# Bilinear gather by matmul: image differences, clamped-ramp weights and 32x32 row sums in place of absolute-distance weights and 128x128 row sums

## The reference

```
py = clip(row + off[..., 0], 0, 31);  px = clip(col + off[..., 1], 0, 31)
out = v00*(1-wy)*(1-wx) + v01*(1-wy)*wx + v10*wy*(1-wx) + v11*wy*wx
```

## Time and profile before

| | us |
|---|---|
| median of 3 runs | 6671.31 (6658.63 to 6683.49) |
| the profiled execution, first to last instruction | 6663.4 |
| TensorE busy (matmuls) | 5906.7 (89%) |
| VectorE busy | 4273.1 (64%) |
| ScalarE busy | 2369.6 (36%) |
| GpSimd busy | 348.5 (5%) |

### The profile page before, as it was taken

One profiled execution on the slowest core, in us unless ns is written; L12 is line 12 of the kernel. 1 busy time (PEld: TensorE's weight loads), 2 busy tenths in 40 slices (PEclk: granted clock), 3 DMA queues, 4 the chain that ended last, 5 costly groups with the idle time before them and its releaser, 6 DMA issues. The chain is left out here.

```text
span 6663.4 us, 63932 instructions
## 1 busy us (share of the span) xinstructions
PE 5906.7 (89%) x22480; PEld 3405.5 (51%) x22528; DVE 4273.1 (64%) x6238; ACT 2369.6 (36%) x2515; POOL 348.5 (5%) x193
## 2 busy tenths in 40 slices
PE   4877888769998999898997999999999969978997
PEld 2333333247776776676774444444444434434442
DVE  5888888856655665221223777778778747746774
ACT  2222222022221221000001666666666626634651
POOL 0222222300000000000000000000000000000000
PEclk7888888679998999999998999999999989989997
DMA  0000000010000000222124002011020060044012
GB/s 27 19 20 19 20 19 19 13 64 13 13 7 20 13 13 24 88 51 64 45 57 108 5 5 69 5 30 46 5 69 5 5 161 23 5 62 95 6 36 84
DMA packets 237972, 242.27 MB, mean 36 GB/s; under 512 B 176425, under 2 KB 178025, under 8 KB 236745
## 3 DMA queue, kind: packets, MB, share of 16 engines
q1 hardware_dynamic: 237640, 237.98, 13.1%
HBM read 137.28 MB, written 100.66 MB: 36 GB/s over the span
## 5 line engine op out<-in xcount | busy, mean ns | idle before, releaser
L1349 ACT ACTIVATE g_wts<-ps,l_index 128x1024 f32<-128x1024 f32 x1536 | 1712.0, 1115 | 1812.3 <-PE ps L1384 1810.4
L1397 PE MATMUL ps<-g_wts,l_img 128*128 128x512 f32 x3072 | 1577.8, 595 | 19.2 <-DMA l_img<-dense 19.1
L1384 PE MATMUL ps<-g_coord,l_spread 128*128 128x512 f32 x3072 | 1479.9, 563 | 107.6 <-DMA g_coord<-coords 106.3
L1369 DVE TENSOR_TENSOR g_prod<-ps,g_wts 128x512 f32<-128x512 f32 x1536 | 1062.7, 692 | 538.2 <-issue 439.5
L1361 DVE TENSOR_SCALAR g_wts<-g_wts 128x1024 f32<-128x1024 f32 x1536 | 1050.4, 684 | 76.2 <-ACT g_wts L1349 76.2
L1384 PEld LDWEIGHTS ps<-g_coord,l_spread 128*128 128x128 f32 x3072 | 556.9, 191 | 986.0 <-issue 567.6
L1279 PE MATMUL ps<-o_pad,o_ow 128*128 128x512 f32 x3456 | 849.9, 408 | 7.7 <-DVE o_pad L821 7.7
L1092 PE MATMUL ps<-l_pair,l_w 128*128 128x512 f32 x3072 | 782.1, 404 | 0.0
L1279 PEld LDWEIGHTS ps<-o_pad,o_ow 128*128 128x128 f32 x3456 | 657.0, 190 | 195.0 <-DVE o_pad L821 7.9
L1397 PEld LDWEIGHTS ps<-g_wts,l_img 128*128 128x128 f32 x3072 | 577.4, 189 | 170.7 <-DMA l_img<-dense 23.4
L1092 PEld LDWEIGHTS ps<-l_pair,l_w 128*128 128x128 f32 x3072 | 576.6, 191 | 157.0 <-issue 29.4
(11 more groups left out here) (240 smaller groups left out, 4312.7 us busy)
## 6 DMA issues: line engine op xcount, KB each, us to landing
coords<-o_parts SPq DMA_DIRECT2D x192, 256.0 KB, 3.8
g_coord<-coords SPq DMA_DIRECT2D x18, 2048.0 KB, 9.6
l_x<-xcur SPq DMA_DIRECT2D x16, 1024.0 KB, 6.3
l_img<-dense SPq DMA_DIRECT2D x96, 128.0 KB, 6.4
gathered<-g_res SPq DMA_DIRECT2D x48, 256.0 KB, 2.0
l_xn<-in_x SPq DMA_DIRECT2D x8, 1024.0 KB, 4.9
l_acc<-in_x SPq DMA_DIRECT2D x8, 1024.0 KB, 4.9
xcur<-l_acc SPq DMA_DIRECT2D x16, 512.0 KB, 2.8
```

The costliest lines, as they stand in the source:

```text
L1349: nc.scalar.activation(wts[:, i % WB, :, :].rearrange("p y n -> p (y n)"), ps[:, lo:lo + 2 * HALF], ACT.Abs, bias=index[:, 0:1]).then_inc( ...
L1369: nc.vector.tensor_tensor(prod[:, k % PB, :], ps[:, (4 + k % 2) * HALF:(5 + k % 2) * HALF], wts[:, k % WB, 1, :], ALU.mult).then_inc(sem(" ...
L1384: ins = nc.tensor.matmul(ps[:, lo:lo + HALF], spread[:, y, g, :], coord[:, s, u, j * HALF:(j + 1) * HALF], start=True, stop=True)
L1397: nc.tensor.matmul(ps[:, lo:lo + HALF], img[:, s, u * NG + g, :], wts[:, i % WB, 0, :], start=True, stop=True).then_inc(sem("rows_summed"), 1)
```

## The change

Weights. The stored image becomes a difference image (second difference over rows and columns, D = d/dy d/dx of x), and the weight of row i becomes a clamped ramp, min(max(py - i + 1, 0), 1), so that sums of differences give the interpolated value. The same holds for columns. GpSimd makes the differences in `build_offsets_1` (four instructions for each channel half, in place before the store) and in `build_middle` (two for each image), and the store to `dense` waits for them.

Gather. The unit is now a quad of 16 channels x 512 pixels, what four steps did; a turn has 64 of them. Channels of a quad are laid out as 4 x 4: strip r (32 partitions) and part c.

- spread: eight matmuls of 64 rows x 128 columns, four for row weights ("k", partitions 0 to 63) and four for column weights ("v", partitions 64 to 127), each into one bank.
- ScalarE makes max(x + bias, 0) of all four v and of k tasks 0 and 1, 128x512 each, through a ring of two banks; VectorE of k tasks 2 and 3 through one bank of its own.
- GpSimd clamps the four k results in SBUF at 1, 128x512 each.
- rows sum: 16 float32 matmuls of 32x32, in two halves of eight (four column strips x two row strips); the results lie in four banks.
- VectorE: min(v, 1) * rows sum, 128x1024 from two banks, one for each half.
- fold: four matmuls, as before, one bank.

The order by turn n on TensorE: spreads for v of quad n+1 (parts 0 and 1), the first for VectorE (k of quad n+2), the fold of quad n-1, spread k of n+2, first half of the rows sums of n+1, spreads v, v and k, the second for VectorE, second half of the rows sums.

Loads of a turn: for each set four coordinate DMAs (512 KB) and four image DMAs (the dense 32 columns of a channel, no zeros around them). Coordinates are stored with one DMA a kind in `build_offsets_1` and with two an image in `build_middle`. The memsets of `load_constants` go.

Core of the diff (stage code of the stores, the coordinate layout and the constants' arrays cut):

```diff
 build_offsets_1
-                            sp.wait_ge(sem("split_ready"), KC * (m + 1))
+                            sp.wait_ge(sem("steps_ready"), KC * (m + 1))
...
+                        pool.wait_ge(sem("split_ready"), KC * (m + 1))
+                        for k in range(KC):
+                            xk = x[:, m % 2, k, :]
+                            link(nc.gpsimd.tensor_copy(down[:, 0:SIDE], xk[:, 0:SIDE]))
+                            link(nc.gpsimd.tensor_tensor(down[:, SIDE:N], xk[:, SIDE:N], xk[:, 0:N - SIDE], ALU.subtract))
+                            rows, to = (v.rearrange("p (y w) -> p y w", w=SIDE) for v in (down[:, :], xk))
+                            link(nc.gpsimd.tensor_copy(to[:, :, 0], rows[:, :, 0]))
+                            nc.gpsimd.tensor_tensor(to[:, :, 1:SIDE], rows[:, :, 1:SIDE], rows[:, :, 0:SIDE - 1],
+                                                    ALU.subtract).then_inc(sem("steps_ready"), 1)
 build_gather, scalar
+                    for n in range(-2, Q):
+                        for task in turn_tasks(n):
+                            kind, q, c = task
+                            a = at[task]
+                            act.wait_ge(sem("ring_filled"), a + 1)
...
+                            nc.scalar.activation(to, bank(a % 2), ACT.Relu, bias=index[:, 0:1]).then_inc(sem("ring_read"), 1)
+                        if n >= QUADS and n % QUADS == 0:
+                            evacuate(n // QUADS - 1)
 build_gather, gpsimd
+                    for q in range(Q):
+                        for c in range(4):
+                            if c in by_dve(q):
+                                pool.wait_ge(sem("dve_read"), dve_at["k", q, c] + 1)
+                            else:
+                                pool.wait_ge(sem("ring_read"), at["k", q, c] + 1)
+                            part = kw[:, q % KB, c, :]
+                            nc.gpsimd.tensor_scalar(part, part, 1.0, 0.0, ALU.min, ALU.max).then_inc(sem("clamped"), 1)
 build_gather, vector
-                            nc.vector.tensor_scalar(wts[:, i % WB, :, :], wts[:, i % WB, :, :], 1.0, -1.0, ALU.min,
-                                                    ALU.add).then_inc(sem("weights_ready"), 1)
...
+                        nc.vector.tensor_scalar(kw[:, q % KB, c, :], bank(DVE_BANK), index[:, 0:1], 0.0, ALU.add,
+                                                ALU.max).then_inc(sem("dve_read"), 1)
...
+                        nc.vector.scalar_tensor_tensor(prod[:, n % PB, 2 * half:2 * half + 2, :].rearrange("p r n -> p (r n)"),
+                                                       vw[:, n % VB, 2 * half:2 * half + 2, :].rearrange("p r n -> p (r n)"),
+                                                       1.0, ps[:, lo:lo + 2 * HALF], ALU.min,
+                                                       ALU.mult).then_inc(sem("weighted"), 1)
 build_gather, tensor
+                        return nc.tensor.matmul(bank(to), spread[y:y + 64, h, c, :],
+                                                coord[y:y + 64, s, t, j * HALF:(j + 1) * HALF], start=True, stop=True)
...
+                    def for_act(task):
+                        a = at[task]
+                        if a >= 2:
+                            pe.wait_ge(sem("ring_read"), a - 1)
+                        spread_step(task, a % 2).then_inc(sem("ring_filled"), 1)
...
+                        if half == 0:
+                            pe.wait_ge(sem("clamped"), 4 * (n + 1))
+                        if n:
+                            pe.wait_ge(sem("weighted"), 2 * (n - 1) + half + 1)
+                        for c in range(4):
+                            for r in (2 * half, 2 * half + 1):
+                                mine = slice(r * SIDE, (r + 1) * SIDE)
+                                lo = (ROW_BANK + r) * HALF
+                                ins = nc.tensor.matmul(ps[c * SIDE:(c + 1) * SIDE, lo:lo + HALF], img[mine, s, g, c, :],
+                                                       kw[mine, n % KB, c, :], start=True, stop=True)
...
+                    for n in range(-2, Q):
+                        act_tasks, tasks = turn_tasks(n), dve_tasks(n)
+                        for task in act_tasks[:2]:
+                            for_act(task)
+                        for task in tasks[:1]:
+                            for_dve(task)
+                        if n >= 1:
+                            fold_step(n - 1)
+                        for task in act_tasks[2:3]:
+                            for_act(task)
+                        if 0 <= n + 1 < Q:
+                            rows_step(n + 1, 0)
+                        for task in act_tasks[3:]:
+                            for_act(task)
+                        for task in tasks[1:]:
+                            for_dve(task)
+                        if 0 <= n + 1 < Q:
+                            rows_step(n + 1, 1)
 build_middle
-                        sp.wait_ge(sem("h_ready"), 4 * (m + 1))
+                        sp.wait_ge(sem("steps_ready"), m + 1)
...
+                        pool.wait_ge(sem("h_ready"), 4 * (m + 1))
+                        link(nc.gpsimd.tensor_tensor(down[:, :, 1:SIDE + 1], stack[0:CM, m, 1:SIDE + 1, 1:SIDE + 1],
+                                                     stack[0:CM, m, 0:SIDE, 1:SIDE + 1], ALU.subtract))
+                        nc.gpsimd.tensor_tensor(step[:, m, :].rearrange("p (y w) -> p y w", w=SIDE), down[:, :, 1:SIDE + 1],
+                                                down[:, :, 0:SIDE], ALU.subtract).then_inc(sem("steps_ready"), 1)
 load_constants
-                nc.gpsimd.memset(c["img"][:, 0:SETS // 2, :, :], 0.0).then_inc(sem("img_zero"), 1)
-                nc.vector.memset(c["img"][:, SETS // 2:SETS, :, :], 0.0).then_inc(sem("img_zero"), 1)
```

More of the change, by code:

```diff
@@ L31 @@
 UNITS = P // BLK
+QUADS = P // (UNITS * 4)
 SETS = 4
@@ L1372, in _ @@
+                    for n in range(-2, Q):
+                        tasks = dve_tasks(n)
+                        if n >= 0:
+                            weigh(n, 0)
+                        for task in tasks[:-1]:
+                            relu(task)
+                        if n >= 0:
+                            weigh(n, 1)
+                        for task in tasks[-1:]:
+                            relu(task)
                 @block.tensor
                 def _(pe):
-                    def spread_step(i):
-                        s, j, g, u = steps[i]
-                        if i < UNITS:
-                            pe.wait_ge(sem(f"first_coord_loaded{u}"), 16)
-                        elif i == per or (s and i % (per * NH) == 0):
-                            pe.wait_ge(sem(f"coord_loaded{s}"), 16)
-                        if i >= 2:
-                            pe.wait_ge(sem("distance_ready"), i - 1)
-                        for y in range(2):
-                            lo = (2 * (i % 2) + y) * HALF
-                            ins = nc.tensor.matmul(ps[:, lo:lo + HALF], spread[:, y, g, :],
-                                                   coord[:, s, u, j * HALF:(j + 1) * HALF],
-                                                   start=True, stop=True)
-                        ins.then_inc(sem("spread_ready"), 1)
@@ L1389, in rows_step @@
-                    def rows_step(i):
-                        s, j, g, u = steps[i]
-                        if i % (per * NH) == 0:
-                            pe.wait_ge(sem(f"img_loaded{s}"), 64)
-                        pe.wait_ge(sem("weights_ready"), i + 1)
-                        if i >= 2:
-                            pe.wait_ge(sem("weighted"), i - 1)
-                        lo = (4 + i % 2) * HALF
-                        nc.tensor.matmul(ps[:, lo:lo + HALF], img[:, s, u * NG + g, :], wts[:, i % WB, 0, :], start=True,
-                                         stop=True).then_inc(sem("rows_summed"), 1)
@@ L1400, in fold_steps @@
-                    def fold_steps(q):
-                        r, g = divmod(q, NG)
-                        pe.wait_ge(sem("weighted"), UNITS * (q + 1))
-                        if g == 0 and r >= 2:
-                            pe.wait_ge(sem("res_ready"), r - 1)
-                        lo = (6 + r % 2) * HALF
-                        for u in range(UNITS):
-                            ins = nc.tensor.matmul(ps[u * BLK:(u + 1) * BLK, lo:lo + HALF], fold[:, g, :],
-                                                   prod[:, (UNITS * q + u) % PB, :], start=(g == 0), stop=(g == NG - 1))
-                        ins.then_inc(sem("folded"), 1)
@@ new lines, in fold_step @@
+                    def fold_step(n):
+                        s, j, g = quads[n]
+                        pe.wait_ge(sem("weighted"), 2 * (n + 1))
+                        if g == 0 and n:
+                            pe.wait_ge(sem("res_ready"), n // QUADS)
+                        for r in range(4):
```

(3 more changed lines are left out.)

214 lines of the change are left out of this document (122 added, 92 removed).

## The result

| us | before | after |
|---|---|---|
| median of 4 runs each | 6669.64 | 8072.16 (8070.4 to 8074.39) |
| ratio, 95% interval | | 1.2101 (1.2084 to 1.2118) |
| profiled execution, first to last instruction | 6663.4 | 8068.9 |
| mean granted TensorE clock | 0.924 | 0.698 |

The change makes the kernel 21% slower, where 2.3% faster was forecast. The time is near that of rival 3, the clock (8120), which had a chance of 0.04.

A forecast was written before the change was run, and what follows sets the result against it. TensorE was taken to bound the gather: 1.51 + 1.80 + 0.90 + 0.96 + 0.75 = 5.92, with dispatch 6.05 us a quad instead of 6.48. 384 quads save 165, the middle costs 13: 6520 us, range 6380 to 6990.

The forecast's parts named there:

- rival 3: TensorE's clock falls to 0.5 in the gather: streams cost 4.2 more, 10.2 us a quad, 8120 us; chance 0.04.
- Row sums, fold: On TensorE per quad: both row-sum halves, eight tiles together, 1.80 us instead of 3.43; fold unchanged at 0.90.
- Rival 2: Row and column strips don't run together, or dispatch at its upper bound: 7.8 us a quad, 7190 us; chance 0.06.
- Dispatch: TensorE's sequencer issues 32 instructions a half: 0.13 us a quad taken; 0.3 late at 0.11 a pair.
- Two banks for ScalarE: On TensorE, the last of three spreads waits for ScalarE's read: 1.18 us instead of 0.43, a stall of 0.75.
- Changes of shape: Six on TensorE a quad instead of two, three at 0.12 us and three at 0.20: 0.96; bounds 0 and 1.26.
- Spreads: Eight 64-row matmuls a quad on TensorE, only one neighbouring pair overlapping: 1.73 - 0.22 = 1.51 us.
- Clamp on GpSimd: Each 128x512 clamp in the gather takes 0.60 us (0.65 with semaphore) and is hidden; ends 0.60 and 1.18.
- GpSimd against VectorE in the middle: In `build_middle`, the difference image's subtracts on GpSimd cost 13 us over four turns; bounds 0 and 75.
- Turn starts: 32 DMAs instead of 24 on SP and a longer prologue: 0 taken, bounds -3 and +5 us a turn.
- Rivals 4 and 5: 4: switches and dispatch cancel the gain, 6690, chance 0.08; 5: more spreads stall on ScalarE's banks, 6760, chance 0.04.
- rival 1: GpSimd's clamp is slow, 1.18 us: first half starts 1.28 later, 7.21 us a quad, 6965 us; chance 0.18.

The follow-up runs named there:

- e1: Changed kernel with every spread widened from 64 to 128 rows, the added weights zero: 6668.63 us; median of ten timed runs 6652.09, ratio 0.9982 to the kernel before.
- e4: Kernel before with only its spreads cut from 128 to 64 rows, the two of a step on different halves of the array: 6836.63 us.
- e2: Changed kernel with each half's eight 32x32 row sums replaced by two 128x128 ones, spreads kept at 64 rows: 7198.1 us.
- e5: Changed kernel with both halves of the row sums issued together at the second half's place, spreads kept at 64 rows: 6244.47 us.
- e7: Changed kernel with only the four row-weight spreads of a quad widened to 128 rows, the four column-weight spreads left at 64: 7610.12 us.
- e9: e6 with one bank instead of two between TensorE and ScalarE, so each spread for ScalarE waits for the last read: 8107.65 us.
- e6: Changed kernel with both halves of the row sums issued together, as in e5, and the 128-row spreads of e1: 6276.4 us.

## Why the prediction was wrong

**The step that failed** is the one that gave the clock no price: the sum was made with streams at full clock, and rival 3 was put at 0.04 with the words "32-column folds leave the granted clock at 1.00 in the groups' windows, and it is 1.00 in a stretch of 64-row pairs; only idle stretches of many us lowered it". What the runs showed in its place is a clock of 0.50 in the gather, which doubles TensorE's part of a quad: 10.22 us for 6.05. The first two rows were read rightly and prove too little. The fold filled the array: 128 rows by four strips of 32 columns, all at once. The stretch of 64-row pairs is 2.3 us of a stage that otherwise runs on 128 rows, and it is 64 rows twice at the same time. Neither shows a loop in which most matmuls leave half of the array idle and which waits as well, and the rival deserved the chance of something unseen. Rival 3's price was right: 10.2 us forecast, 10.22 measured; 8120 forecast, 8072 measured.

The third clause is wrong, and the trace of the kernel before says so. In its expert layer the clock falls while TensorE's records are busy without a gap (a row of the timeline, then the windows on either side of the fall):

```profile
1486.96 4.05 PE L1063 MATMUL ps<-l_gate_w,l_xn 128*128 128x8 f32 x32
...
1483.00:1490.00 7.00, 7.00 (x46) 6.23 (x45) 6.79 (x8) 0.99 (x2) 0.00 (x0) 1.00 0.01 2
1490.00:1496.80 6.80, 6.80 (x20) 5.54 (x20) 1.37 (x3) 0.43 (x1) 0.00 (x0) 0.50 0.00 0
```

What stands ahead of the fall is a run of 32 matmuls that stream 8 columns each. It falls in the same way, at 0 idle, behind such runs at 1640, 2125 and 2275. So a busy share of 100% and a fall to 0.50 were on view together before the forecast.

The other steps, most of them read from the run with 128-row spreads, where the clock is 1.00:
- *Row sums, fold:* a half with its change of shape back takes 3800.43 - 3799.41 = 1.02, where the steps gave 0.90 + 0.20; fold and change 1.00, the same sum. Right, a little high. Rival 2 is refuted.
- *Dispatch:* no late half is seen; the quad of e1 is filled without the 0.13.
- *Two banks for ScalarE:* from the first spread of the stretch to the third it is 3805.05 - 3803.77 = 1.28 instead of 0.43, so the stall is 0.85, not 0.75. ScalarE's read with bias lasts 0.683 to 0.687, where the evacuation's 0.59 was taken; that is the 0.1. The trace before had reads of that shape with a bias too, at 0.686 to 0.688 (L438).
- *Changes of shape:* what is left of e1's quad is 6.29 - 1.73 - 1.80 - 0.90 - 0.85 = 1.01, so 0.17 each where 0.12 and 0.20 were taken (mean 0.16); 0.19 each in e4. Nearly right.
- *Spreads:* the lost overlap in that run costs 0.22. With it the forecast would be 6.05 + 0.22 = 6.27, and 6.29 was measured. That it is so close is in part luck: 0.10 too little for the stall and 0.05 for the changes are made up by the 0.13 of dispatch. Each term held within about 0.1.
- *Clamp on GpSimd,* called the decisive one with a chance of 0.18 for its rival: 0.613, as forecast at 0.60 from the copy and the memset. Three in a row take 1.77 and end before the first half needs them. The loop of 512 elements that the Trainium skill (GPSIMD Engine Reference, Performance versus the Vector engine) has at 768 ns is not this instruction, and its figure didn't apply. The attention went to the wrong unknown.
- *VectorE:* relu 0.75 for 0.69, product 1.21 for 1.28. Never the bound.
- *GpSimd against VectorE in the middle:* 18 us for both stages, 13 forecast. Below.
- *Turn starts:* the forecast was 0, with bounds of -3 and +5 us a turn. From the first spread to the first fold of a turn it is 21.7 us, 17.2 before, so +4.5 at half clock; near the bound. It is inside the 6 x 231.3 above.
- *Offsets 1 and constants:* 0 forecast; the first spread starts at 3616.6, at 3616.8 before. Right.
- *Rivals 4 and 5* did not come about: e1's quad at full clock is below 6.48. By its own terms rival 5 comes to 6750 and not 6760, and rival 1, counted from 6.05 instead of 5.92, to 7.34 us a quad and 7015.

**Would the forecast have held at full clock?** Not as a time. The run with wide spreads holds the clock, and gives 6652 where 6520 was forecast. 384 x (6.29 - 6.05) = 92 of the 132 us are its own price, 5 the middle stages; some 35 stay, probably for turn starts, where quads of 10.67 are seen at a low clock. What the change itself would take at full clock, no run can tell, since it has the full clock for some 3 us at a time and never for a whole quad.

**What stays open.** That the narrow tiles' small use of the array is the cause is shown by e1 and e2, which widen one kind of matmul each and keep the waits and the changes of shape; e5 and e7 fit. That it is the use over time is argued: e9 shows that idle time counts as well, and its order against the changed kernel fits no plain average. How the chip weighs rows, columns and idle time against each other the runs don't tell. The dips at the starts of turns (0.86 and 0.87 in windows at a start in e5, 0.91 in e1) begin in the 12 us in which TensorE waits for the loads; why some starts then take one slow quad and others eight was not tried. Nor was whether the changed loop would keep the full clock if a turn began with it; at 3858 it lost it within a quad.

## What to carry to other kernels

Before a matmul is cut into narrow tiles, ask how much of TensorE's array will be at work over the whole loop, waits included, and not only how long the records will be: tiles that leave rows or strips idle kept the clock only where the rest of the loop filled the array (e2, e4) or the work was packed closer (e5). Read the granted clock of the loop first in the profile after; a busy share near 100% says nothing of it. And look in the trace before for every fall of the clock, not only for those behind idle time. If narrow tiles are wanted, issue all that fit the array together (sixteen took 1.14 us, eight 1.09), which saves changes of shape too, at nearly 0.2 us each.

## What the runs showed of the hardware

- **The clock falls, and stays low, without an idle stretch.** It falls behind gaps of 0.54 us at most in the changed kernel (3858) and in e7 (4360), and with no gap at all in the kernel before (1490); it is 0.50 over 1754 us with TensorE's records busy 93% of it. The same matmuls packed closer run at 1.00 (e5), and those of e6 spread out do not (e9, 0.79).
- **A change of tile shape costs TensorE 0.17 (e1) to 0.19 us (e4),** so that pairing 64-row spreads, two at a time between 128-row matmuls, loses: 6.93 for 6.48 us a group.
- **GpSimd and VectorE hold each other up in SBUF.** The timeline of a middle stage of the changed kernel:

```profile
6289.50 2.48 POOL L1659 TENSOR_TENSOR o_down<-o_stack 64x1024 f32<-64x1024 f32 x1 [12.14 <-ACT o_stack L1675]
6290.15 3.05 DVE L822 TENSOR_TENSOR o_pair<-o_stack,o_pair 128x1156 fp32r<-128x1156 f32 x1
6292.06 2.89 POOL L1661 TENSOR_TENSOR o_step<-o_down 64x1024 f32<-64x1024 f32 x1
6293.12 2.45 DVE L821 CAST o_pair<-o_stack 128x1156 fp32r<-128x1156 f32 x1
```

  VectorE's subtract took 1.36 before and takes 3.05 beside GpSimd's; the cast takes 2.45, where one that began before GpSimd's instruction takes 0.76. The Trainium skill (SBUF — State Buffer, Who interferes with whom) calls the shared ports an exclusive lock held for a whole instruction; the trace agrees: the subtract ends 1.22 and the second cast 0.62 after the GpSimd instruction beside it. In the gather, where VectorE's operands lie in PSUM on one side, its times don't vary beside 1536 clamps (0.750 to 0.752 for all 768 reads).
- **ScalarE's read of 128x512 from PSUM** takes 0.685 us with a bias and relu, 0.59 as a plain copy.
